# Weight loads of an attention kernel issued from SyncE's queue instead of ScalarE's

## What is computed

```python
mod = (_silu(L0_c) @ L0_wmod).reshape(L0_c.shape[0], 6, 1, -1)   # sa, ca, ga, sb, cb, gb
h = _layernorm(x, axis=-1) * (1 + ca) + sa
x = x + ga * attention(h)
h = _layernorm(x, axis=-1) * (1 + cb) + sb
x = x + gb * ffn(h)

# attention: B=4, S=512, D=256, NUM_HEADS=16, HEAD_DIM=128
w = codes * jnp.repeat(scales, 32, axis=0)        # for each of wq, wk, wv, wo
q, k, v = h @ wq + bq, h @ wk + bk, h @ wv + bv
attn = softmax(q k^T / sqrt(128), axis=-1)
out = (attn v) @ wo + bo

# ffn: x @ W.T plus a LoRA of rank 16, of 8 experts, the 2 best by a softmax router
```

## Time and profile before

| | |
|---|---|
| median of 3 runs | 881.12 us (880.6 to 881.14) |
| the profiled execution, its own time | 881.12 us |
| its span, first to last instruction | 879.0 us |
| around the span | 2.1 us |
| PE busy | 823.7 us (94%) |
| DVE, POOL, ACT busy | 617.1, 404.1, 381.8 us |
| DMA queue of SP (q1) | 74.02 MB |
| DMA queue of ACT (q10) | 16.26 MB |

### The profile page before, as it was taken

One profiled execution on the slowest core, in us unless ns is written; L12 is line 12 of the kernel. 1 busy time (PEld: TensorE's weight loads), 2 busy tenths in 40 slices (PEclk: granted clock), 3 DMA queues, 4 the chain that ended last, 5 costly groups with the idle time before them and its releaser, 6 DMA issues.

```text
span 879.0 us, 13011 instructions
## 1 busy us (share of the span) xinstructions
PE 823.7 (94%) x3548; PEld 607.9 (69%) x3548; DVE 617.1 (70%) x1268; ACT 381.8 (43%) x852; POOL 404.1 (46%) x439
## 2 busy tenths in 40 slices
PE   3969899999999999999999999999999999998758
PEld 2746677777777777777777777777777777665556
DVE  3767676776777777777767777777777775767563
ACT  2543544444444445544444444544444443442321
POOL 4433355444544555445544554445545552433230
PEclk9999899999999999999999999999999999999889
DMA  6143334443344334443444335533443353333002
GB/s 199 50 111 109 80 83 106 130 123 93 90 131 134 94 89 113 138 118 88 112 132 115 89 89 140 140 88 89 130 133 98 90 154 94 76 84 78 19 1 96
DMA packets 73808, 90.61 MB, mean 103 GB/s; under 512 B 19571, under 2 KB 40501, under 8 KB 73781
## 3 DMA queue, kind: packets, MB, share of 16 engines
q1 hardware_dynamic: 55988, 74.02, 32.9%
q10 hardware_dynamic: 17792, 16.26, 6.2%
HBM read 21.01 MB, written 2.10 MB: 26 GB/s over the span
## 4 chain that ended last, share of the span: by engine, by line
PE 74%; SPq 8%; issue 6%; DVE 5%; POOL 3%; DMA 2%; ACT 2%; POOLq 0%; ACTq 0%; DVEq 0%
PE o_odd L938 12%; PE o_even L938 11%; PE score L878 8%; PE score L880 8%; PE score L879 8%; SPq L281 7%; PE qv L878 5%; PE qv L880 5%; PE qv L879 5%; PE ky L878 3%; PE ky L879 3%; PE ky L880 3%; POOL prob L364 2%; DVE neg_max L741 2%; DMA pT<-pB 1%
## 5 line engine op out<-in xcount | busy, mean ns | idle before, releaser
L364 POOL TENSOR_TENSOR prob<-prob,inv_sum 128x512 f32<-128x512 f32 x256 | 258.5, 1041 | 385.2 <-DVE inv_sum L746 384.9
L741 DVE TENSOR_REDUCE neg_max<-score 128x1 f32<-128x512 f32 x256 | 176.0, 691 | 195.7 <-PE score L880 195.4
L488 ACT ACTIVATE prob<-score,neg_max 128x512 f32<-128x512 f32 x256 | 175.6, 688 | 59.4 <-DVE neg_max L741 59.2
L752 DVE STREAM_TRANSPOSE pB<-prob 128x512 f32<-128x512 f32 x256 | 179.7, 703 | 8.8 <-POOL prob L364 1.0
L878 PE MATMUL score<-k_hi,q_hi 128*128 128x512 f32 x256 | 124.7, 487 | 6.6 <-ACT hT_hi L431 6.4
L938 PE MATMUL o_even<-pT,v 128*128 128x512 f32 x256 | 115.5, 593 | 1.9 <-DMA pT<-pB 1.9
L938 PE MATMUL o_odd<-pT,v 128*128 128x512 f32 x256 | 115.6, 594 | 1.6 <-DMA pT<-pB 1.6
L880 PE MATMUL score<-k_hi,q_lo 128*128 128x512 f32 x256 | 101.4, 396 | 0.0
L879 PE MATMUL score<-k_lo,q_hi 128*128 128x512 f32 x256 | 100.5, 393 | 0.0
L450 ACT ACTIVATE v<-qv 128x512 f32<-128x512 f32 x64 | 38.2, 597 | 134.9 <-PE qv L880 134.9
L701 DVE TENSOR_TENSOR yT<-score,yT 128x512 f32<-128x512 f32 x121 | 77.2, 676 | 3.9 <-PE score L880 3.9
(11 more groups left out here) (205 smaller groups left out, 1471.6 us busy)
## 6 DMA issues: line engine op xcount, KB each, us to landing
pT<-pB SPq DMA_DIRECT2D x1024, 64.0 KB, 2.0
out_dram<-x_nat SPq DMA_DIRECT2D x8, 256.0 KB, 2.1
stage<-in_L_attn_wv_codes_dram ACTq DMA_DIRECT2D x7, 256.0 KB
stage<-in_L_attn_wv_scales_dram ACTq DMA_DIRECT2D x14, 128.0 KB
stage<-in_L_attn_wq_codes_dram ACTq DMA_DIRECT2D x7, 256.0 KB
stage<-in_L_attn_wq_scales_dram ACTq DMA_DIRECT2D x14, 128.0 KB
stage<-in_L_attn_wk_codes_dram ACTq DMA_DIRECT2D x7, 256.0 KB
stage<-in_L_attn_wk_scales_dram ACTq DMA_DIRECT2D x14, 128.0 KB
```

The costliest lines, as they stand in the source:

```text
L364: pool.tensor_tensor(prob[:, i], prob[:, i], inv_sum[:, i:i + 1].to_broadcast([P, S]), ALU.mult).then_inc(prob_ok, 1)
L488: act.activation(prob[:, i], score_ps[i][:, :], ACT.Exp, bias=neg_max[:, i:i + 1], accum_out=row_sum[:, i:i + 1]).then_inc(exp_ok, 1)
L741: dve.tensor_reduce(neg_max[:, i:i + 1], score_ps[i][:, :], AX.X, ALU.max, negate=True).then_inc(max_ok, 1)
L752: dve.transpose(pB[:, s % 2, :, i].rearrange("p g k q -> p k g q"), prob[:, i].rearrange("p (k g q) -> p k g q", k=QT, g=G)).then_inc(pB_o ...
```

## The change

SP issues all loads that ACT issued, after the train of a step: those of `v` and `q` for the next pass after step 0, of `k` after step 1, of `o` after step 2, each after the same wait for `w_ok[m]`, now on SP. In pass 7 SP issues `wmod_2` and `w_raw` after the train of step 0, `a_raw` and `g_raw` after that of step 1, `b_raw` after that of step 2. ACT keeps `scale_codes` at the end of step 2 and issues no DMA any more. The loads of `b_raw` now count on the semaphore `ld_ffn`, so that PE waits for them one step earlier, in `ffn_dense_weights` instead of `ffn_lora_weights`. The sizes and shapes of all transfers are as before. Cut to its core:

```diff
--- before.py
+++ after.py
@@ sync engine's block @@
+            def load_weights(m, p):
+
+                if m == "o":
+                    rows = CODES[m].rearrange("(h p) d -> p h d", p=P)
+                    sp.dma_start(codes[m][:, :, :], rows[:, bass.ds(2 * p, 2), :]).then_inc(ld_w[m], 16)
+                    for j in range(2):
+                        start = 2 * NB * D * p + j * NB * D
+                        src = bass.AP(SCALES[m].tensor, start, [[D, NB], [0, BLK], [1, D]])
+                        sp.dma_start(scales[m][:, j], src).then_inc(ld_w[m], 16)
+                    return
...
+            def next_weights(m, p):
+
+                sp.wait_ge(w_ok[m], (1 if m == "v" else 2) * p)
+                load_weights(m, p)
 
             def pair(p, first=False, last=False):
                 for s in range(SPP):
@@ -280,6 +285,27 @@
                         for g in range(G):
                             sp.dma_start(flat(pT32[32 * g:32 * (g + 1), par, a]),
                                          flat(pB[32 * a:32 * (a + 1), par, g])).then_inc(p_land[par], 16)
+                    if last:
+                        if s == 0:
+                            for m in "vqk":
+                                sp.wait_ge(w_ok[m], (1 if m == "v" else 2) * PAIRS)
+                            sp.dma_start(wmod_2, cols[:, :, GA * P:MODS * P]).then_inc(ld_wmod2, 16)
+                            sp.dma_start(w_raw, ffn_w.rearrange("(c p) d -> p c d", p=P)).then_inc(ld_ffn, 16)
+                        elif s == 1:
+                            sp.dma_start(a_raw, lora_a.rearrange("e r d -> (e r) d")).then_inc(ld_ffn, 16)
+                            sp.dma_start(g_raw, gate_w).then_inc(ld_ffn, 16)
+                        elif s == 2:
+                            sp.wait_ge(w_ok["o"], 2 * PAIRS)
+                            for c in range(O // P):
+                                sp.dma_start(b_raw[:, c], lora_b[:, c * P:(c + 1) * P, :].rearrange("e p r -> p e r")).then_inc(ld_ffn, 16)
+                    elif s == 0:
+                        next_weights("v", p + 1)
+                        next_weights("q", p + 1)
+                    elif s == 1:
+                        next_weights("k", p + 1)
+                    elif s == 2:
+                        next_weights("o", p + 1)
+
             pair(0, first=True)
@@ scalar engine's block @@
                         act.wait_ge(bias_ok, 2 * p + 3)
-                    if not last and s < 4:
-                        m = "vqko"[s]
-                        act.wait_ge(w_ok[m], (1 if m == "v" else 2) * (p + 1))
-                        load_weights(act, m, p + 1)
-                        if s == 2:
-                            scale_codes(p + 1)
-                    if last and s == 0:
-                        for m in "vqk":
-                            act.wait_ge(w_ok[m], (1 if m == "v" else 2) * PAIRS)
-                        act.dma_start(wmod_2, mod_cols[:, :, GA * P:MODS * P]).then_inc(ld_wmod2, 16)
-                        act.dma_start(w_raw, ffn_w.rearrange("(c p) d -> p c d", p=P)).then_inc(ld_ffn, 16)
-                    if last and s == 1:
-                        act.dma_start(a_raw, lora_a.rearrange("e r d -> (e r) d")).then_inc(ld_ffn, 16)
-                        act.dma_start(g_raw, gate_w).then_inc(ld_ffn, 16)
-                    if last and s == 3:
-                        act.wait_ge(w_ok["o"], 2 * PAIRS)
-                        for c in range(O // P):
-                            act.dma_start(b_raw[:, c], lora_b[:, c * P:(c + 1) * P, :].rearrange("e p r -> p e r")).then_inc(ld_b, 16)
+                    if s == 2 and not last:
+                        scale_codes(p + 1)
 
@@ tensor engine's block @@
 
-                pe.wait_ge(ld_ffn, 16 * 3)
+                pe.wait_ge(ld_ffn, 16 * (3 + O // P))
...
             def ffn_lora_weights():
 
-                pe.wait_ge(ld_b, 16 * (O // P))
```

More of the change, by code:

```diff
@@ L170, in bass_adaln_mxfp4_attention_moe_lora_kernel @@
             sem(n) for n in ("ld_c", "c_tr", "ld_vec", "vec_tr", "vec_ok", "ld_wmod", "ld_wmod2", "ld_ffn"))
-        ld_x_first, ld_b = sem("ld_x_first"), sem("ld_b")
+        ld_x_first = sem("ld_x_first")
         ld_x = [sem(f"ld_x{b}") for b in range(B)]
@@ L199, in bass_adaln_mxfp4_attention_moe_lora_kernel @@
         hw_ok, hw_tr, hwT_ok, res_ok, stored = (sem(n) for n in ("hw_ok", "hw_tr", "hwT_ok", "res_ok", "stored"))
-        mod_cols = wmod.rearrange("(c p) n -> p c n", p=P)
         CODES = dict(q=wq_codes, k=wk_codes, v=wv_codes, o=wo_codes)
@@ L236, in turned @@
             return pT32[:, par, :, :, kt, :].rearrange("p a i q -> p i a q")
[L238 to L253, removed]
         block = ctx.enter_context(nc.Block())
@@ L263, in _ @@
             sp.dma_start(x_nat[:, 2:QT], first[:, 2:QT]).then_inc(ld_x[0], 16)
-            sp.dma_start(wmod_1, mod_cols[:, :, 0:GA * P]).then_inc(ld_wmod, 16)
+            cols = wmod.rearrange("(c p) n -> p c n", p=P)
+            sp.dma_start(wmod_1, cols[:, :, 0:GA * P]).then_inc(ld_wmod, 16)
+            def load_weights(m, p):
[7 more added lines that the diff above has]
+                    return
+                cols = CODES[m].rearrange("(c p) f -> p c f", p=P)
+                sp.dma_start(codes[m][:, :, :], cols[:, :, bass.ds(PW * p, PW)]).then_inc(ld_w[m], 16)
+                for c in range(DC):
+                    start = PW * p + c * NB * FEAT
+                    src = bass.AP(SCALES[m].tensor, start, [[FEAT, NB], [0, BLK], [1, PW]])
+                    sp.dma_start(scales[m][:, c], src).then_inc(ld_w[m], 16)
             for m in "qkv":
-                load_weights(sp, m, 0)
+                load_weights(m, 0)
             for i, vec in enumerate((bq, bk, bv, bo)):
@@ L271, in _ @@
                 sp.dma_start(x_nat[:, b * QT:(b + 1) * QT], x[b].rearrange("(t p) d -> p t d", p=P)).then_inc(ld_x[b], 16)
-            load_weights(sp, "o", 0)
+            load_weights("o", 0)
+            def next_weights(m, p):
+                sp.wait_ge(w_ok[m], (1 if m == "v" else 2) * p)
+                load_weights(m, p)
             def pair(p, first=False, last=False):
```

## The result

| | before | after |
|---|---|---|
| median of 4 runs each, on one chip | 881.13 us (880.6 to 883.42) | 909.55 us (905.98 to 910.58) |
| ratio | | 1.031, 95% interval 1.0276 to 1.0344 |
| the profiled execution, its own time | 881.12 us | 908.02 us |
| its span | 879.0 us | 906.1 us |

The change makes the kernel 3.1% slower: the right side, but outside the range (884 to 904), and the loss of about 28 us is more than twice the 10.4 forecast.

A forecast was written before the change was run, and what follows sets the result against it. PE was taken to bound the loop, waiting once SP's queue exceeds free time and slack. 10.8 + 1.2 + 1.3 - 2.5 - 0.4 = + 10.4 us on 881.12 gave 891.5 us, 1.2% slower, range 884 to 904.

The forecast's parts named there:

- free time and slack: SP is free 1.70 us in each step; a train lands 0.50 us before PE would have to wait.
- The price of a load on SP: Loads in the loop hold SP 3.7 us after step 0, 1.8 after step 1, 1.9 after step 2: 10.8 us in all.
- Trains slowed by the loads: Trains of sixteen starts on SP slowed by a megabyte ahead of them: 0.2 us a pass, + 1.2 us.
- Stray starts in pass 1: One long start in each train of steps 1 and 3, now without slack: + 1.3 us.
- The old waits, - 2.5: PE's 2.5 us of waits in the loop's six passes before the change, replaced by the new ones.
- Passes 0 and 7: Moved starts fit on SP outside the loop, and a train loses its neighbour: - 0.2 us each, - 0.4 together.
- No wait of SP for `w_ok`, no data late, ACT's gain nothing: SP's moved waits block nothing, loads reach their readers in time, and freeing ACT of its starts gains nothing.
- Rival 1: Six starts take less than 2.2 us on SP and PE never waits: 878.5 us; chance 4%.
- Rival 2: Six loads in a row fill SP's queue and the later ones cost more: 905 us; chance 7%.
- Rival 3: PE's wait once a pass brings matmuls at the lower clock, + 18 us: 909 us; chance 6%.
- The signs of being wrong: No PE wait in passes 2 to 6; starts under 0.37 us; trains over 11 us every pass; PEclk under 1.00.
- The rule of the skill: About 50 ns to dispatch a DMA on another path: 0.3 us after step 0, so no wait.

The follow-up runs named there:

- sp_four: The changed kernel with one load on SP after each of steps 0 to 3 (v, q, k, o): 897.82 us, ratio 1.0175 to before.
- sp_spaced: The changed kernel with the loads of v, q, k, o on SP after steps 0, 1, 3 and 5: 890.1 us, ratio 1.0092 to before.
- ko_on_sp: The kernel before with only the loads of k and o on SP, after steps 1 and 2: 892.51 us, ratio 1.0119.
- vq_on_sp: The kernel before with only the loads of v and q on SP, both after step 0: 921.57 us, ratio 1.0468.
- split_train: The changed kernel with four of each train's sixteen DMA starts given to ACT: 879.03 us, ratio 0.9959 to before.
- sp_few_bytes: The changed kernel with the same starts, each loop load bringing an eighth of its bytes to an unread buffer: 904.54 us, ratio 1.0264 to before.
- act_gap: The kernel before with ACT's loads moved in front of the activation of v in its queue: 895.65 us, ratio 1.0171.

## Why the prediction was right in kind and wrong in size

- **What bounds the kernel, free time and slack: right.** 1.70 and 0.50 us give, with the measured lengths, the passes of sp_four, sp_spaced and ko_on_sp and pass 6 of vq_on_sp to 0.1 us. And for after: with the measured lengths pass 3 of after is 4.67 + 2.23 + 2.39 - 3 x 1.70 - 0.50 = 3.7 us, plus 0.4 for trains of 10.22, 10.08 and 10.10 us, 4.1 in all; measured 97.85 - 93.71 = 4.14.
- **The price of a load on SP: the step that failed.** The forecast took ACT's prices, each from the first start to the end of the last, with 0.05 us between two. v and q took 4.67 instead of 3.7, k 2.23 instead of 1.8, o 2.39 instead of 1.9: 1.9 us a pass too little. About half of it is time around the loads, which holds the queue as well: 0.62, 0.26 and 0.32 us where the forecast had 0.10, 0.05 and 0.05. The other half are starts that took longer on SP than on ACT, q's last (0.94) the longest. Even the upper end of the price, from the earlier trace rows, was 4.2 and 1.9, below what was measured, and so the range ended too low. Free time and slack are subtracted from the price, and so a fault of a quarter doubled the result: 7.4 - 5.6 = 1.8 us a pass forecast, 9.3 - 5.6 = 3.7 found.
- **Trains slowed by the loads**: 0.4 a pass instead of 0.2. Together with the prices 2.1 us a pass, in six passes 12.8.
- **Stray starts in pass 1**: forecast + 1.3, found 2.5 over the other passes. Step 1's train has one start of 1.20 us, and PE waits 3.41 us; step 3's has one of 1.93, larger than in the earlier trace rows, lands 3.35 us after its last start, and PE waits 0.81 where pass 2 has nothing. The excess is there in sp_four, sp_spaced and ko_on_sp too (4.4, 2.8 and 2.6 over theirs), and absent in split_train: its pass 1 has starts of 2.46 and 1.44 us, and slack hides them. In the twelve traces all starts of `pT <- pB` on SP above 1.1 us stand in passes 0, 1 and 7, except for one each in pass 4 of before and of sp_spaced. Passes 0 and 7 are written out and pass 1 is the first turn of the loop, so each of the three runs its code for the first time; passes 2 to 6 run it again. No run tests whether that is the reason.
- **The old waits, - 2.5: right**, they were replaced: passes 2 to 6 of after are within 0.5 us of each other.
- **Passes 0 and 7**: - 0.4 forecast; found - 0.7 in pass 0 and + 1.8 in pass 7 and behind it. At least a part of the 1.8 is the clock behind the small matmuls (seven follow each other every 0.43 us instead of 0.23, 1.4 us), which shows without the moved loads too.
- **The sum with the measured sizes**: 10.4 + 12.8 + 1.2 (pass 1) + 1.5 (passes 0 and 7) = 25.9, against 26.9 between the two profiled executions. The missing 1.0 is what passes 2, 4, 5 and 6 take more than pass 3, 0.1 to 0.5 each.
- **No wait of SP for `w_ok`, no data late, ACT's gain nothing: right.** On the chain SP goes from its last `pT` start through register steps to the first load without a stop; ACT is busy 381.4 us (381.8 before), and no other engine's work moved.
- **Rival 1 (fits in the gap)** is excluded by 4.67 against 2.20. **Rival 2 (a backlog)** gave nearly the right time, 905, for a wrong reason: only q's last start (0.85 to 0.98 us, other starts of scales about 0.6) is stretched in every pass, by 0.2 to 0.4, and in passes 1 and 4 the one before it too. sp_few_bytes takes seven eighths of the bytes away and keeps 2.6 of the 3.1%. **Rival 3 (the clock)** happened, in four passes of six, and cost about 0.3 us a time in after; its price per fall was read as 3 us and is 1.5 to 2.4 where it is paid. That its 909 us is the measured time is luck. The condition set for it, a wait above 2.2 us, was met since the wait became 2.3 to 3.4 us; but behind 2.52 (pass 3) and 3.02 us (pass 4) it did not fall. When it falls stays open.
- **The signs of being wrong**: one of the four came, PEclk under 1.00 in the loop. It told of the longer wait and not of another cause. The passes (97.9 us and more, for 95.5 to 96), the long wait (2.3 and more, for 1.5) and the six starts (4.23 from the first start to the last end, for 3.2 to 4.2) lay above what was named as right.
- **The rule of the skill**: by the 50 ns of the Trainium skill, page "DMA: Bandwidth & Descriptors", section "Anatomy of one DMA — SWDGE (gpsimd) path", there would have been no wait. In the loop of after the starts of the loads on SP took 0.38 to 0.98 us. The same page of the Trainium skill says, in "Rules for kernel authors", that spreading DMAs over several engines saves only the issue time of a sequencer. The runs agree, and show that this can be all that matters: between after and split_train, with the same bytes, lie 30.5 us.

## What to carry to other kernels

Before DMA starts go to another queue, compare what that queue has free in a step with the whole time they hold it: read from the end of the instruction ahead to the start of the one behind, not from the first start to the end of the last. Where the time is short, a fault of a quarter in the price can double the loss, since free time and slack are subtracted first; give the price a range of that size. And where a queue is the bound, move starts off it (four of sixteen were enough) rather than gather more on it; the queue that takes them needs room at that very place.

## What the runs showed of the hardware

- The start of a DMA on SP held its queue for a time that hardly depended on the bytes (q's last start, above, is the exception): 0.38 to 0.53 us for codes of 256 KB and for an eighth of them, about 0.6 for scales of 128 KB and for an eighth of them, 0.59 for 64 KB within the chip. Single starts took 1.1 to 2.8 us, nearly all in passes 0, 1 and 7.
- A load that ACT started from 1.4 us before to 0.12 us behind the last start of a train delayed the landing of that last DMA, to 2.85 to 4.99 us from its start against 2.0 in the earlier trace rows (eleven trains of the loop in act_gap and vq_on_sp). Started 0.18 to 0.20 us behind it, the load delayed nothing (pass 6 of vq_on_sp, 2.02; five trains of act_gap, 2.0). It is not the only condition: in split_train, with no load on ACT, the trains behind the loads land late too (2.8 to 4.2 us in passes 2 to 6), and its slack hides it. Moving a transfer out of one collision put it into another, twice.
- The granted clock fell in some passes of one execution and not in others with waits as long, and a lower level is not always a loss: where waits would follow anyway it cost 0.3 us (sp_few_bytes, pass 3), elsewhere 1.5 (vq_on_sp, passes 3 and 5).
